# A min-GRU whose candidate's negative branch is formed on ScalarE as the sigmoid of a clipped argument, with VectorE's minimum dropped

## What is computed

```python
def _log_g(x):
    return jnp.where(x >= 0.0, jnp.log(jax.nn.relu(x) + 0.5), -jax.nn.softplus(-x))
...
for W in (W0, W1):
    z = jnp.einsum('bth,hk->btk', h, W)
    hidden, gate, proj = jnp.split(z, 3, axis=-1)
    log_coeffs = -jax.nn.softplus(gate)
    log_values = -jax.nn.softplus(-gate) + _log_g(hidden)
    out = _heinsen_scan(log_coeffs, log_values)
    g = jax.nn.sigmoid(proj)
    h = g * out + (1.0 - g) * h
```

## Time and profile before

| | |
|---|---|
| median of 3 runs | 1729.43 us (1729.08 to 1729.48) |
| the profiled execution | 1724.85 us, its span 1723.1 us |
| mean granted TensorE clock | 0.922 |
| busy over the span | PE 81%, DVE 72%, ACT 63%, POOL 54% |
| pipeline of `min_gru` in the trace | first matmul at 29.22 us, last instruction (POOL L292) from 121.89 us to 123.15 us |

### The profile page before, as it was taken

One profiled execution on the slowest core, in us unless ns is written; L12 is line 12 of the kernel. 1 busy time (PEld: TensorE's weight loads), 2 busy tenths in 40 slices (PEclk: granted clock), 3 DMA queues, 4 the chain that ended last, 5 costly groups with the idle time before them and its releaser, 6 DMA issues. The chain is left out here.

```text
span 1723.1 us, 24398 instructions
## 1 busy us (share of the span) xinstructions
PE 1399.7 (81%) x8211; PEld 753.0 (44%) x8230; DVE 1233.5 (72%) x1774; ACT 1088.5 (63%) x1857; POOL 929.0 (54%) x484
## 2 busy tenths in 40 slices
PE   6748089767767888888888668999999999999987
PEld 2315078622223333333333335555555555555553
DVE  2974133237789989998989189878787878787863
ACT  4423045358856666665666257888888888888873
POOL 0430623300498888787887056655555556565641
PEclk9866589878789999999999789999999999999999
DMA  1006311220000000003000011111111111121110
GB/s 62 0 3 104 106 53 49 61 59 1 3 0 1 1 1 0 1 1 128 1 1 1 15 42 27 44 26 44 26 44 26 44 25 44 32 50 32 38 26 25
DMA packets 48848, 53.56 MB, mean 31 GB/s; under 512 B 10419, under 2 KB 32101, under 8 KB 48358
## 3 DMA queue, kind: packets, MB, share of 16 engines
q1 hardware_dynamic: 46438, 47.46, 11.2%
q0 software_dynamic: 2304, 4.74, 0.8%
HBM read 19.63 MB, written 9.47 MB: 17 GB/s over the span
## 5 line engine op out<-in xcount | busy, mean ns | idle before, releaser
L1147 POOL TENSOR_TENSOR ssm_dbu<-ssm_dtu,ssm_b_all 128x1024 f32<-128x1024 f32 x128 | 299.2, 2359 | 40.1 <-ACT ssm_b_all L1071 39.8
L1778 POOL TENSOR_TENSOR at_direct<-at_direct,home_dt 128x1024 f32<-128x1024 f32 x64 | 152.4, 2382 | 307.8 <-DVE home_dt L1868 307.8
L934 PE MATMUL ssm_bank<-ssm_seen,ident 128*128 128x512 f32 x512 | 251.1, 614 | 35.5 <-POOL ssm_seen L1156 33.3
L1065 ACT ACTIVATE ssm_bank<-home_dt,ssm_decay 128x512 f32<-128x512 f32 x256 | 173.5, 691 | 71.8 <-DVE ssm_state L1254 70.6
L1254 DVE TENSOR_TENSOR_SCAN ssm_state<-ssm_bank,ssm_dbu 128x512 f32<-128x512 f32 x128 | 149.1, 1209 | 20.5 <-POOL ssm_dbu L1147 13.6
L1254 DVE TENSOR_TENSOR_SCAN ssm_state<-ssm_bank,ssm_carry,ssm_dbu 128x512 f32<-128x512 f32 x128 | 156.5, 1269 | 6.8 <-ACT ssm_bank L1065 4.0
L934 PEld LDWEIGHTS ssm_bank<-ssm_seen,ident 128*128 128x128 f32 x512 | 97.9, 195 | 121.7 <-issue 67.9
L1071 ACT ACTIVATE ssm_b_all<-ssm_bank 128x512 f32<-128x512 f32 x128 | 75.7, 591 | 101.2 <-PE ssm_bank L911 77.9
L1559 PE MATMUL at_two<-home_u,at_hs 128*128 128x512 f32 x256 | 129.2, 628 | 9.6 <-ACT at_kT L1706 5.6
L1783 POOL TENSOR_TENSOR home_u<-home_u,at_inv 128x1024 f32<-128x1024 f32 x64 | 121.5, 1898 | 18.6 <-DVE at_inv L1879 18.6
L1789 POOL TENSOR_TENSOR at_direct<-at_direct,at_rnorm 128x1024 f32<-128x1024 f32 x64 | 123.2, 1924 | 0.2
(11 more groups left out here) (241 smaller groups left out, 3375.0 us busy)
## 6 DMA issues: line engine op xcount, KB each, us to landing
at_v_mix<-at_v SPq DMA_DIRECT2D x112, 128.0 KB, 2.3
at_hs<-branch SPq DMA_DIRECT2D x64, 128.0 KB, 2.3
moe_w<-in_moe_w SPq DMA_DIRECT2D x16, 256.0 KB
moe_to_experts<-moe_empty SPq DMA_DIRECT2D x10, 258.0 KB, 8.0
moe_slot_rows<-moe_to_experts SPq DMA_DIRECT2D x10, 258.0 KB, 2.8
x<-in_x SPq DMA_DIRECT2D x8, 256.0 KB, 3.4
moe_rows<-moe_from_experts SPq DMA_DIRECT2D x8, 256.0 KB, 4.6
home_dt<-in_turn SPq DMA_DIRECT2D x2, 1024.0 KB
```

The source lines that it names most:

```text
L934: last = nc.tensor.matmul(bank[Y0 + half][:], ident[:], seen[:, n % 2, half], start=False, stop=n == STATES - 1)
L1065: nc.scalar.activation(bank[DA0 + half][:], chunk_of(dt[:, half], t), ACT.Exp, scale=decay[:, half, n:n + 1]).then_inc(r[f"da{half}"], 1)
L1147: nc.gpsimd.tensor_tensor(dbu[:, i % RING], dtu[:, t % 2], b_all[:, i % 2:i % 2 + 1, :].broadcast_to([P, 2, CH]), ALU.mult).then_inc(r["db ...
L1778: nc.gpsimd.tensor_tensor(direct[:, n % TURNED], direct[:, n % TURNED], crossed[:, n % 2], ALU.add).then_inc(s["added"], 1)
```

## The change

ScalarE forms the negative branch by itself, as sigmoid(-relu(-hidden)) = sigmoid(min(hidden, 0)), in two activations: Relu of the negated hidden into `cand`, and, after `update`, the sigmoid of the negated `cand` in place. A semaphore `below` orders the two. The four sigmoids that stood in a loop stand one by one. VectorE's minimum and its semaphore `low` are dropped; L320 now waits for `cand` and follows directly.

```diff
-        names = "gates cand update gate keep low fed value scan off gated h".split()
+        names = "gates below cand update gate keep fed value scan off gated h".split()
...
-            prime(act, "cand update gate keep")
+            prime(act, "below cand update gate keep")
...
-                        for to, name, g, scale in ((cand, "cand", 0, 1.0), (update, "update", 1, 1.0),
-                                                   (gate, "gate", 1, -1.0), (keep, "keep", 2, 1.0)):
-                            nc.scalar.activation(to[:, layer, k], bank[layer][g][:], ACT.Sigmoid, scale=scale
-                                                 ).then_inc(s[name][layer], 1)
+
+                        nc.scalar.activation(cand[:, layer, k], bank[layer][0][:], ACT.Relu, scale=-1.0
+                                             ).then_inc(s["below"][layer], 1)
+                        nc.scalar.activation(update[:, layer, k], bank[layer][1][:], ACT.Sigmoid
+                                             ).then_inc(s["update"][layer], 1)
+                        act.wait_ge(s["below"][layer], done(t))
+                        nc.scalar.activation(cand[:, layer, k], cand[:, layer, k], ACT.Sigmoid, scale=-1.0
+                                             ).then_inc(s["cand"][layer], 1)
+                        nc.scalar.activation(gate[:, layer, k], bank[layer][1][:], ACT.Sigmoid, scale=-1.0
+                                             ).then_inc(s["gate"][layer], 1)
+                        nc.scalar.activation(keep[:, layer, k], bank[layer][2][:], ACT.Sigmoid
+                                             ).then_inc(s["keep"][layer], 1)
...
-            prime(dve, "low fed value scan gated h")
+            prime(dve, "fed value scan gated h")
...
-                    nc.vector.tensor_scalar(cand[:, layer, k], cand[:, layer, k], 0.5, None, ALU.min
-                                            ).then_inc(s["low"][layer], 1)
-                    dve.wait_ge(s["low"][layer], done(t))
```

## The result

The changed kernel takes 1732.33 us in the median of 20 runs (1729.15 to 1733.76), the kernel before 1729.01 in 20 runs on the same chips (1727.58 to 1731.83). The ratio is 1.0016, with a 95% interval of 1.0010 to 1.0022: slower by 2.8 us (1.7 to 3.8 by the interval); the two medians are 3.3 apart. That is clear of no difference at all, and by its middle inside the 0.2% that the prediction counts as no change; the interval's upper end lies just above it. The forecast of +2.05 lies in the interval.

The account below looks back on a forecast made before the run. The prediction took turns between VectorE and GpSimd to bound the loop. Its terms, +0.96 + 1.41 + 0.54 - 0.95 + 0.09 = +2.05 us on 1729.43, gave 1731.5 us, range 1728.7 to 1734.2.

Parts of the forecast that it names:

- The ring of two engines: Pipeline loop: VectorE and GpSimd instructions taking turns bound the step, so dropping the minimums gains 0.19 us a step.
- Rival C: Steps 3 to 7: VectorE's work is the bound, each step gains 1.91 us; total -6.6 us, 1722.9; chance 0.07.
- Steps 3 to 7: Four loop steps plus step 3: dropping the minimums gains 0.19 us each, 0.95 us in all.
- Two more activations ahead of PE: Steps 0 and 1: PE waits for ScalarE's last read, one activation later each, 0.96 us lost.
- the bare load: Start: sigmoid's table load falls behind the Relu and the wait for the gates, unhidden, 1.41 us lost.
- D: Start: the table load drains ScalarE too, priced as a second load-time; +3.3 us, 1732.8; chance 0.03.
- B: Start: the table load is hidden, ahead of the Relu or in PE's first tile; +0.64 us, 1730.1; chance 0.09.
- Step 2: Layer 1's first candidate comes later, the minimum's 0.46 us already taken off; 0.54 us lost.
- Step 9 and the end: Last step: gates 0.45 us earlier, candidate 1.00 later, minimum's 0.46 gone; +0.09 us.
- PE's clock: Second and last tiles of gates: speed level may cost or gain up to 0.95 us; taken as 0.
- E: Start: PE falls to its slow level in both tiles and layer 1's first gates; +6.7 us, 1736.1; chance 0.10.
- The prediction's own signs: Wrong if the step falls to 9 us, the load is at stage start, or step 1 and 2 tiles exceed 5 us.

Follow-up runs that it names:

- no_add: The changed kernel without GpSimd's addition of layer 1's output to x (first residual left out); ratio to the kernel before 0.9985.
- sub_on_dve: The changed kernel with the table set loaded ahead, both subtractions moved from GpSimd to VectorE's step end, layer 1's addition first; ratio to the kernel before 0.9983.
- act_alone: The changed kernel with VectorE's minimum and its semaphore added again, so only ScalarE's part of the change is in; ratio to the kernel before 1.0034.
- preload: The changed kernel with sigmoid's table set asked for at the head of ScalarE's stream; ratio to the kernel before 1.0008.
- the second trace: The changed kernel profiled once more with no edit; first matmul to last instruction 96.35 us, against 96.72 in its first trace.
- sub_late: As sub_on_dve, with layer 0's feed also moved behind the additions from step 3 on; ratio to the kernel before 0.9977.

## Why the prediction held

- **The ring of two engines**, and not VectorE's busy time, bounds the loop: shown by `no_add`, where the pair behind the addition falls from 2.10 to 1.28, and by `sub_on_dve`, where the multiplications fall from 2.34 to 1.28. Rival C is out: 9.64 and 9.49 us a step, not 7.9.
- **Steps 3 to 7**, forecast as -0.95: from the scans of step 2 to those of step 7 it is 47.66 in place of 48.69, so -1.03; -1.06 from `act_alone`.
- **Two more activations ahead of PE**, forecast as +0.96 for steps 0 and 1, and **the bare load**, +1.41: the second tile starts 1.92 later relative to the first (1.89 forecast), and `preload` takes off 1.41. The third starts 3.21 later: the 1.92, the 0.77 of PE's clock named below, and 0.52 for the second activation. The load costs its 1.28 and the lost overlap, with no drain behind it: 35.08 is 0.01 after its end, so D is out, and B as well.
- **Step 2**, forecast as +0.54: the scans start 3.75 later relative to the first tile, 0.54 more than the third tile's 3.21.
- **Step 9 and the end**, forecast as +0.09: from step 7's scans to the last instruction 21.78 against 21.71, +0.07.
- **PE's clock**, taken as 0 with the ends -0.95 and +0.95: the second tile took 0.77 more, and 0.64 in the second trace. This is the one term that was clearly off, and it lies within its end. With it, 2.05 + 0.77 = 2.82, against 2.79 in the trace and 2.8 by the ratio. The fall of E to three tiles did not come: the third tile took 4.51 and the first gates of layer 1 2.74, as before. The granted clock (the column before the last two) of the second tile, in the kernel before and then in the changed one:

```profile
35.98:40.49 4.51, 4.51 (x6) 1.47 (x6) 1.52 (x2) 0.00 (x0) 1.26 (x1) 0.62 0.00 0
```

```profile
37.31:42.59 5.28, 5.28 (x6) 1.82 (x6) 1.56 (x2) 0.00 (x0) 1.26 (x1) 0.53 0.00 0
```

The prediction's own signs caught this in part. It would have been wrong if PE's tiles of steps 1 and 2 took over 5 us; the one of step 1 did, with 5.28, the one of step 2 did not. The third tile was to come 2.4 us later and came 3.21 later, the scans of step 2 2.9 and came 3.75. The load near 34.4 (33.79, in a trace whose first tile starts 0.59 us earlier), the idle time ahead of L335 (0.52 for about 0.4) and VectorE's busy share in the loop (0.948) came as said. The mechanism was forecast, then, and the time was 1732.33 for 1731.5. The base was 1729.01 in place of the 1729.43 that the forecast started from; with that, the medians' difference is 3.3 and not 2.05, and the clock's term is most of what is missing.

What stays open is why the level falls in one tile and not in another. After an idle time of 4.18 us (4.30 in `act_alone`) the second tile was slow in all of the changed kernel, its repeat, `act_alone` and `no_add` (5.15 to 5.46); after 2.76 it took 4.40 in `preload` and `sub_late` and 5.46 in `sub_on_dve`; after 2.25 it took 4.15 to 4.51 in six traces. That the longer gap causes the 0.77 is what these rows suggest, not what they show.

## What to carry to other kernels

Busy time of an engine can be standing: compare an instruction's duration with its shortest, and look at what ends just before it does. Taking work out of an engine whose neighbours stand for another engine mostly moves the standing, here all but 0.2 us of 1.9 a step. The worth of such an edit depends on the order around it: with GpSimd's subtractions taken over by VectorE, and the feeds beside its addition, the same edit was worth 1.8 to 2.0 a step, half of it because the minimum would have stood for that addition. That order alone, with the minimum, was no gain (1.0022); only the two together were (0.9977). A new first activation that does not need the new table set pulls the load out of its cover: ask for the set by hand (1.41 us in the trace).

## What was not expected of the hardware

- The same idle time of PE went with tiles of 4.40 and 5.46 us (2.76 us idle), and of 4.51 and 2.81 (2.25 us idle, granted clock 0.62 and 1.00).
- Two profiles of one program, equal to 0.03 us over the first pipeline, were 5.7 us apart some 260 us later; 4.0 of them arose in the mixture of experts.
- A sigmoid from SBUF took 0.62 to 0.63 us, one from PSUM 0.59 to 0.62.
